# Copying a pair's token numbers and gates behind the choice of experts and the pick, in a fused graph and mixture-of-experts kernel

## What is computed

```python
xn = layernorm(x)
mean = segment_sum(xn[src], dst) / maximum(count(dst), 1)
x2 = x + relu(relu(mean @ Wl.T + bl + xn @ Wr.T) @ Wln.T + xn) + mix(xn)
z = layernorm(x2)
shared = gelu(z @ W1s + b1s) @ W2s + b2s
gates = top2_renormalised(softmax(z @ Wr))
routed = sum_e gates[e] * (gelu(z @ W1p[e] + b1p[e]) @ W2p[e] + b2p[e])
out = x2 + shared + routed
```

## Time and profile before

| | |
|---|---|
| median of 3 runs | 2691.06 us (2684.02 to 2691.8) |
| the profiled execution | 2688.45 us, of it the span 2686.7 us |
| granted TensorE clock over the span | 0.957 |
| VectorE busy | 1060.6 us, 3479 instructions |
| gathers L521 | 1568, busy 1562.3 us |
| comparisons L870 | 225, 1094 ns each |
| pair_in's first copy L1048 | 39, idle before them 311.0 us |

### The profile page before, as it was taken

One profiled execution on the slowest core, in us unless ns is written; L12 is line 12 of the kernel. 1 busy time (PEld: TensorE's weight loads), 2 busy tenths in 40 slices (PEclk: granted clock), 3 DMA queues, 4 the chain that ended last, 5 costly groups with the idle time before them and its releaser, 6 DMA issues.

```text
span 2686.7 us, 51843 instructions
## 1 busy us (share of the span) xinstructions
PE 2346.5 (87%) x12344; PEld 2023.5 (75%) x12345; DVE 1060.6 (39%) x3479; ACT 801.9 (30%) x1897; POOL 1847.6 (69%) x1790
## 2 busy tenths in 40 slices
PE   0688867778779999999999999999999999988998
PEld 0455556666668888888888888888888888877887
DVE  8545443333344343433434343343434334332221
ACT  1233312222223232323333232323323233223332
POOL 2677767777777777777777777777777777751221
PEclk9899978888889999999999999999999999988999
DMA  8333333343345564655556565555656556545764
GB/s 277 87 105 101 107 108 111 107 115 111 103 152 175 146 181 141 182 160 161 176 146 180 141 181 154 168 175 148 180 142 182 151 171 178 147 146 146 216 178 110
DMA packets 256254, 405.91 MB, mean 151 GB/s; under 512 B 70073, under 2 KB 187001, under 8 KB 255578
## 3 DMA queue, kind: packets, MB, share of 16 engines
q0 software_dynamic: 95360, 232.54, 32.2%
q1 hardware_dynamic: 154218, 164.36, 19.0%
q10 hardware_dynamic: 6384, 6.42, 0.7%
HBM read 362.16 MB, written 41.01 MB: 150 GB/s over the span
## 4 chain that ended last, share of the span: by engine, by line
POOL 31%; PE 30%; issue 20%; DMA 7%; DVE 7%; DVEq 2%; POOLq 1%; ACT 0%; SPq 0%; PEldq 0%
POOL region L521 27%; PE p_agg L1408 11%; DMA out_rows<-wkv_s,stok_s 4%; PE p_h L1743 3%; PE p_h L1620 3%; POOL slot_d L543 3%; PE p_y L1594 3%; PE p_agg L1769 2%; DMA region<-xn_d,idx_s 2%; PE p_y L1631 1%; POOL out_rows L552 1%; DMA late<-slot_d 1%; PE p_h L1588 1%; PE p_y L1769 1%; PE p_a L1620 1%
## 5 line engine op out<-in xcount | busy, mean ns | idle before, releaser
L521 POOL DMA_INDIRECT region<-xn_d,idx_s x1568 | 1562.3, 996 | 542.0 <-issue 466.9
L1408 PE MATMUL p_agg<-region,onehot 128*128 128x258 f32 x3136 | 813.7, 416 | 137.9 <-DMA region<-xn_d,idx_s 123.5
L1408 PEld LDWEIGHTS p_agg<-region,onehot 128*128 128x128 f32 x3136 | 639.9, 208 | 261.7 <-issue 132.3
L870 DVE TENSOR_TENSOR onehot<-row_s,iota_s 128x896 f32<-128x896 f32 (+1 forms) x225 | 246.2, 1094 | 172.2 <-issue 169.1
L1631 PE MATMUL p_y<-region 128*128 128x256 f32 x1248 | 282.3, 379 | 0.0
L876 DVE TENSOR_TENSOR late<-late,p_agg 128x258 f32 x176 | 74.6, 424 | 477.4 <-issue 242.7
L696 ACT ACTIVATE work<-p_h,b1s_s 128x128 f32<-128x128 f32 x392 | 112.0, 368 | 503.4 <-PE p_h L1588 503.4
L1631 PEld LDWEIGHTS p_y<-region 128*128 128x128 f32 x1248 | 236.9, 190 | 32.5
L1620 PE MATMUL p_h<-wkv_s,region 128*128 128x256 f32 x936 | 218.1, 383 | 0.8 <-ACT wkv_s L683 0.8
L1594 PE MATMUL p_y<-w2s_s,work 128*128 128x256 f32 x768 | 199.4, 382 | 14.8 <-DVE wkv_s L1088 14.8
L1620 PEld LDWEIGHTS p_h<-wkv_s,region 128*128 128x128 f32 x936 | 174.8, 190 | 23.3 <-issue 1.0
(11 more groups left out here) (256 smaller groups left out, 2900.0 us busy)
## 6 DMA issues: line engine op xcount, KB each, us to landing
region<-in_w1p SPq DMA_DIRECT2D x55, 1024.0 KB, 6.6
region<-in_w2p SPq DMA_DIRECT2D x55, 1024.0 KB
region<-xn_d,idx_s POOLq DMA_INDIRECT x1568
rows_s<-slot_d SPq DMA_DIRECT2D x39, 258.0 KB
region<-in_x SPq DMA_DIRECT2D x7, 896.0 KB, 5.2
xn_d<-region ACTq DMA_DIRECT2D x7, 896.0 KB, 6.6
rows<-in_x SPq DMA_DIRECT2D x49, 128.0 KB
xnr_s<-xn_d SPq DMA_DIRECT2D x49, 128.0 KB
```

Of the source, the lines that this page charges most:

```text
L521: pool.indirect_dma_start(out=ring[b][:, u, 0:D], out_offset=None, in_=xn_d, in_offset=IND(ap=idx_s[b][:, u:u + 1], axis=0)).then_inc(s_ro ...
L870: return V.tensor_tensor(out, to, rows, ALU.is_equal)
L1408: m = mm(p_agg[b % 2], onehot[:, b % 2, u, :], ring[b][:, u, :], start=u == 0, stop=u == U - 1)
```

## The change

In the loop's steps and in the late step, VectorE does `pair_in` behind `choose` and `pick`, where it stood ahead of `choose`. The register move that keeps the pair's expert (e_now from e_next, before pick loads the next) is taken out of `pair_in` and stands between choose and pick. The closing step keeps its order.

```diff
             def pair_in():
 
                 dve.reg_add(pairs, pairs, 1)
-                dve.reg_mov(e_now, e_next)
                 k = dve.snap(pairs, min_val=1, max_val=PAIRS)
                 dve.wait_ge(S["const"], 3)
                 dve.wait_ge(S["rows"], 16 * k)
...
                 tables()
+                dve.reg_mov(e_now, e_next)
                 pair_in()
                 pair_out()
...
                 def routed():
                     p = dve.snap(p_r, min_val=1, max_val=NT - 1)
+                    choose(p)
+                    dve.reg_mov(e_now, e_next)
+                    only(unpicked, lambda: pick(p))
                     only(unpaired, pair_in)
-                    choose(p)
-                    only(unpicked, lambda: pick(p))
                     only(unpaired, pair_out)
                     position(p)
...
                 def enter(p):
                     mean(p, edges)
-                    only(unpaired, pair_in)
 
                 def select(p):
                     choose(p)
+                    dve.reg_mov(e_now, e_next)
                     only(unpicked, lambda: pick(p))
+                    only(unpaired, pair_in)
```

## The result

The changed kernel takes **2705.04 us** (median of 5 runs, 2700.89 to 2711.64), the kernel before 2687.94 (5 runs, 2682.48 to 2691.8). By the medians it is 17 us slower, where 21 were forecast. The ratio of the runs is 1.0075, with a 95% interval of 1.0058 to 1.0091, that is 16 to 24 us. The profiled execution took 2705.04 us, 16.6 us of span more than that of before.

What follows compares the result with a forecast made beforehand. POOL's gathers were taken as the bound. The third comparison adds 21 us, all other terms 0: 2688.45 + 21 = 2709.5, said as 2712 against the median; range 2670 to 2728, the main case's own 2697 to 2728.

Steps and rivals of the forecast that it cites:

- The bound: Pair stage, 800 to 2380 us: POOL, issuing gathers without standing still, sets the time at 42.74 us a step.
- choose and pick, cost nothing: VectorE: both, 3.55 us together, run inside its present 7.91 us wait for the scatter-add; the logits must be there.
- sel_s earlier, worth nothing: PE loses its wait for the count and a slower sum, 3.4 us a step, worth nothing at the end.
- Hot 3: Third comparison (L870) starts just ahead of POOL's fourth gather and stretches it: 0.56 us a step, 21 us slower.
- L876 as a witness: VectorE's L876, reading PSUM and SBUF, stretches no gather: an overlapping gather at 1540.46 takes 0.95 us.
- The other comparisons: The first, second and fourth L870 comparisons of a step: taken as 0, with 0.35 us a step either way, 13 us.
- Hot 4: Fourth comparison of a step, 7.67 us behind the third: a stretch of 0.15 us, against 0.08 today.
- Hot 1: First comparison of a step, about 4.07 us after the fourth sum's start; with the second: 0, 13 us either way.
- hot 2: Second comparison of a step, 13.3 us after the first; the two together: 0, 0.35 us a step either way.
- Hot 3 stays clear: Rival: the third comparison starts 0.02 us later than reckoned and misses the gather; 13 us faster, 2678; chance 0.27.
- PE is the bound: Rival: PE sets the time, so 3.4 us in each of 34 steps come back; 116 us, 2575; chance 0.05.
- Nothing moves: Rival: PE's gain is hidden and the comparisons' places average out; 2691; chance 0.08.

Runs made afterwards that it cites:

- the half change: Against the kernel before: choose first, then pair_in's copies, then pick; 2682.28 us, ratio 0.9987.
- The run with 0.16 us more: Changed kernel plus one increment of VectorE's own semaphore and a register operation between pair_in's copies and finish 1; 2676.12 us, 0.9964 of the kernel before.
- the last delay run: Kernel before, all comparisons but the third reading PSUM, plus a 128x400 fill and one semaphore increment behind pick; 2643.76 us, ratio 0.9845.

## Why the prediction was right

*The bound.* POOL's gathers, by the page (18.2 of 16.6 us) and by the table above. "POOL's gaps still 0.3 us at most": right.

*choose and pick, cost nothing; sel_s earlier, worth nothing.* Right: PE's wait for sel_s is gone, the third sum takes 3.21 us (forecast 3.1), and the half change has both for no gain. One cover was thinner than I wrote. The logits are not always there: choose waits 86.6 us for them in 30 steps, out of VectorE's wait for the scatter, which is 191 us and not the "some 250" forecast. Of the two waits named for PE, that for gathered rows came (85.6 us) and that for pair_out did not: PE's row for it has gone.

*Hot 3.* The step with the sum in it. Forecast: 1.50 us behind the end of the copies, 0.05 to 0.06 us ahead of the fourth gather, 0.91 us in four steps of five. Measured in the step shown: 1.47 us behind the end of L1048 (1540.13 to 1541.60), 0.08 ahead, and 0.88 to 0.91 us of hold in 30 of 35 steps. The other 5, whose group straddles two tiles, cost 0.43, as forecast; I had reckoned with a fifth of the steps (and, in the expectations, with 7). From the timelines of 35 steps (each gather's time over 0.946 us, put down to the comparison that ran at its start), hot 3 went from 0.21 to 0.83 us a step: 0.62, forecast 0.56. The mechanism was read rightly, and that the place came out is in part luck. The leads were 0.047 to 0.087 us, and below 0.045 a gather goes free (last section). A hot 3 later by 0.04 us would have let every one of those gathers go, and my own bounds on the 0.65 us ahead of L876 ran from 0.45 to 1.15. The chances, 0.60 against 0.27, said as much.

*L876 as a witness.* The prediction took from one pair that L876, with one input in PSUM, stretches nothing: the gather at 1540.46 and the L876 at 1541.26. That pair can't show it, since there the gather starts first, and by the prediction's own formula nothing that starts later holds it. Other pairs do: over the twelve traces 126 gathers started under an L876 where the rule for held gathers (last section) asked for more than 0.04 us, and they took at most 0.033 us over 0.946.

*The other comparisons.* Mis-sized, within their bounds. Hot 4 rose by 0.16 us a step, forecast 0.07: in 11 of 35 steps it costs over 0.4, against 2 before. One of them:

```profile
1029.69 1.09 DVE L870 TENSOR_TENSOR onehot<-row_s,iota_s 128x896 f32<-128x896 f32 x1 [2.32 <-issue]
1029.78 1.82 POOL L521 DMA_INDIRECT region<-xn_d,idx_s  x1 [0.30 <-issue]
```

I had taken hot 4 as fixed 7.67 us behind hot 3; where it waits for a sum or its group straddles, it is not. Hot 1 fell by 0.14 (forecast 0, with 0.35 a step for hot 1 and hot 2 together either way), hot 2 rose by 0.02. What all gathers together take over 0.946 us, held by a comparison or not, rose by 0.61 us a step (1.27 to 1.88), and a step is 0.60 us longer (42.745 to 43.349). Over 38 steps that is 23 us; 17 arrived in the time. Between 800 and 2380 us the gathers' time over 0.946 us rose by 21 (1033.8 less 1021 of them, against 1028.9 less 1038 of them), and outside it fell by 3.

*The rivals.* "Hot 3 stays clear" needed hot 3 only some hundredths of a microsecond later. The run with 0.16 us more is that case made real: 2676.12, where the rival said 2678. "PE is the bound" fell with the half change: the wait of the matmul engine was taken away and the time didn't move. The rule of the Trainium skill (Perfetto Trace Analysis, Optimization Strategies) that was set beside it speaks of engines that block the critical path; that wait turned out not to lie on it, so the rule as it stands is not contradicted. "Nothing moves", the Trainium skill's sentence on shared interfaces read by itself, fell by the order of work alone making 17 us.

## What to carry to other kernels

Where an engine with many short instructions is short of time, look at the spread of one instruction's duration and not only at the waits: here a median of 0.946 us and a maximum of 1.86 said that something else holds it, and the timeline at its start said what. Taking the collision away (one of the two SBUF inputs moved to unused PSUM columns) was worth 60 us and left 2.6 us of the 17 that this change of order costs. Without that, an edit ahead of a comparison can move the time by tens of microseconds, whatever it was meant for: 0.16 us of work that nobody needs made the changed kernel 29 us faster.

## What the runs showed of the hardware that was not expected

**The hold has a sharp edge and a fixed end.** Over the six traces in which all comparisons read SBUF, a gather that started 0.001 to 0.044 us behind a comparison's start was never held (42 gathers), and one that started 0.045 to 0.9 us behind it always was (882). A held gather ended 1.91 us after the comparison's start, 0.82 after its end, whatever the lead (grouped by lead, the means are 1.912 to 1.915). So a thousandth of a microsecond decides over 0.9 us. In the free cases at the edge it is the comparison that takes longer, 1.12 us at the smallest lead and 1.17 at the largest, for 1.09 (1.16 in the step at 1374.45 above).

**Other operations hold too, for as long as they run.** With all comparisons in PSUM, gathers were still held in the kernel before:

```profile
923.47 0.42 DVE L1192 TENSOR_TENSOR work<-xnr_s,b_s 128x256 f32<-128x256 f32 x1
923.51 1.19 POOL L522 DMA_INDIRECT region<-xn_d,idx_s  x1 [0.30 <-issue]
```

L1192 (L1188 in the kernel before as it stands) has both inputs in SBUF and takes 0.42 us; the gather is held for 0.25 us and ends 0.82 us after it, as with the comparison. I took the gathers that started at least 0.1 us behind the start of such an operation where an end 0.82 us after the operation's meant a hold of over 0.04 us. In the twelve traces there are 335 of them at the four 128x256 operations with both inputs in SBUF (L1188, L1192, L1197 and L1205 of the kernel before), and all 335 were held. The second SBUF input is not the whole of it: L1088, which reads one SBUF tensor and a scalar a row and does 128x256 in 0.35 us, held 245 of 245 such gathers. One is in the step of the earlier trace rows, where the gather starts under the second of the two L1088:

```profile
1543.90 0.62 DVE L1088 TENSOR_SCALAR wkv_s<-wkv_s,gate_s 128x256 f32<-128x256 f32 x2
1544.33 1.01 POOL L521 DMA_INDIRECT region<-xn_d,idx_s  x1 [0.30 <-issue]
```

L1208, with one SBUF input and 0.43 us, held none of 144. What L1088 has in common with the others was not tested.

**A few instructions elsewhere move a comparison by 0.3 us.** In the kernel before, choose starts 1.15 us behind the copies. With comparisons reading PSUM and two more VectorE instructions far ahead, outside the loop, to fill the PSUM copy:

```profile
1500.04 0.19 DVE L1053 COPY gate_s<-rows_s 128x2 f32<-128x2 f32 x1
1501.18 0.17 DVE L1154 COPY rt_s<-p_c 128x8 f32<-128x8 f32 x1 [0.95 <-DVE gate_s L1053]
```

it starts 0.95 us behind them. In the kernel before, one pair of neighbouring register instructions between the two has a hole of 0.42 us, and with the edit that hole is not there (the register instructions' starts are 1535.37 and 1535.84, against 1500.64 and 1500.71). A part of it comes back ahead of them: the first instruction behind the copies starts 0.23 us after their end, for 0.04 before. In all hot 3 moved from 11.13 to 10.8 us, which spoilt the last delay run. In this stretch the two programs have the same instructions; that the place of the code in memory makes the hole is a guess, and it was not tested. Whoever times an edit in such a kernel times this as well.
